# Linear attention beside an FP4 feed-forward, one core: x's transposes on the DMA queue instead of TensorE, and three elementwise jobs off VectorE

## What is computed

```
xn = layernorm(x)                       # x: 8 sequences x 2048 tokens x 256
qkv = xn @ W_qkv.T                      # 16 heads of 16
q = softmax(q over the head) * 16**-0.5;  k = exp(k)
# buckets of 64 tokens: each bucket's q meets the running sums over all earlier buckets
den  = q . cumsum(sum k);  context = cumsum(k^T v);  attn = (q @ context) / max(den, 1e-6)
attention = attn @ W_out.T
# fp4: blocks of 16 are divided by their scale (max|.|/6), rounded to the E2M1 grid, multiplied back
gate, up = fp4(xn) @ fp4(w_gate).T, fp4(xn) @ fp4(w_up).T     # 704 columns each
down = fp4(silu(gate) * up) @ fp4(w_down).T
out = x + attention + down
```

## Time and profile before

| | |
|---|---|
| time, median of 3 runs | 1378.86 us (1377.84 to 1379.21) |
| profiled execution: its time, its span | 1378.78 us, 1377.1 us |
| TensorE matmul busy | 1301.7 us, 95% |
| VectorE busy | 1294.4 us, 94% |
| ScalarE busy | 1028.2 us, 75% |
| GpSimd busy | 250.1 us, 18% |
| granted TensorE clock, mean | 0.989 of full |
| DMA engines, mean busy share | 39.6% in the main queue |

### The profile page before, as it was taken

The page is one execution under the profiler, slowest core; times in us unless marked ns, Lnnn a source line. Parts: engine busy times, 40 slices in busy tenths (PEclk is TensorE's granted clock), DMA queues, the critical chain, the costliest instruction groups (busy, mean ns, idle before and its releaser), DMA issues.

```text
span 1377.1 us, 41687 instructions
## 1 busy us (share of the span) xinstructions
PE 1301.7 (95%) x10318; PEld 913.1 (66%) x10318; DVE 1294.4 (94%) x3901; ACT 1028.2 (75%) x3349; POOL 250.1 (18%) x664
## 2 busy tenths in 40 slices
PE   0279999999999999999999999999999999999996
PEld 0257676677767677676767677676766767676674
DVE  6769999999999999999999999999999999999996
ACT  1577778777787878777787877778787777878772
POOL 2211212111121211112121111112111111212110
PEclk9889999999999999999999999999999999999998
DMA  4023444444344444334444433434444343434334
GB/s 124 4 38 64 91 89 84 88 93 87 78 102 87 84 89 95 83 80 95 92 85 88 97 83 81 99 85 84 88 98 89 76 96 85 92 81 99 81 69 89
DMA packets 362747, 116.85 MB, mean 85 GB/s; under 512 B 327772, under 2 KB 362204, under 8 KB 362716
## 3 DMA queue, kind: packets, MB, share of 16 engines
q1 hardware_dynamic: 361990, 115.80, 39.6%
q10 hardware_dynamic: 726, 0.72, 0.2%
HBM read 19.99 MB, written 16.78 MB: 27 GB/s over the span
## 4 chain that ended last, share of the span: by engine, by line
PE 92%; DVE 4%; ACT 1%; issue 1%; DMA 1%; SPq 0%; DVEq 0%; ACTq 0%
PE outp L1168 11%; PE nump L1118 6%; PE unit1a L1058 6%; PE unit0a L1058 6%; PE outp L1170 5%; PE unit1a L1060 5%; PE unit1a L1062 5%; PE unit0a L1060 5%; PE unit0a L1062 5%; PE ctxp L1128 4%; PE unit1b L1058 4%; PE unit1b L1060 4%; PE unit1b L1062 4%; PE unit0b L1058 4%; PE unit0b L1060 4%; PE unit0b L1062 4%
## 5 line engine op out<-in xcount | busy, mean ns | idle before, releaser
L1168 PE MATMUL outp<-w_down_cat,q_rows 128*128 128x256 f16 x1408 | 246.0, 274 | 0.0
L599 ACT ACTIVATE snap<-ctxp,mask 64x68 f32<-64x68 f32 x1024 | 236.1, 308 | 3.2
L409 POOL TENSOR_TENSOR var_scaled<-squares,var_mul 128x1 f32<-128x1 f32 x128 | 33.5, 262 | 947.8 <-ACT scratch L492 947.8
L1168 PEld LDWEIGHTS outp<-w_down_cat,q_rows 128*128 128x128 f16 x1408 | 138.3, 98 | 16.5
L1170 PE MATMUL outp<-w_down_lo,q_rows 128*128 128x256 f16 x640 | 147.6, 274 | 0.0
L517 ACT ACTIVATE xnt<-trp 128x256 f16<-128x256 f32 x256 | 97.3, 380 | 58.5 <-PE trp L1082 58.5
L562 ACT ACTIVATE th<-unit1a,c_g 128x352 f32<-128x352 f32 x128 | 70.9, 554 | 83.8 <-PE unit1b L1062 83.8
L562 ACT ACTIVATE th<-unit0a,c_g 128x352 f32<-128x352 f32 x128 | 71.0, 555 | 83.0 <-PE unit0b L1062 81.8
L810 DVE TENSOR_REDUCE blk<-h 128x44 f32<-128x704 f32 x128 | 123.8, 967 | 0.1
L863 DVE TENSOR_TENSOR hx_v<-h,blk 128x704 f32<-128x704 f32 x128 | 112.1, 876 | 0.0
L400 POOL TENSOR_TENSOR att_s<-att,att_s 128x256 f16<-128x256 f32 x128 | 86.5, 676 | 124.2 <-ACT att_s L554 124.2
(11 more groups left out here) (203 smaller groups left out, 4156.4 us busy)
## 6 DMA issues: line engine op xcount, KB each, us to landing
xring<-x SPq DMA_DIRECT2D x128, 128.0 KB, 2.7
out<-xring SPq DMA_DIRECT2D x128, 128.0 KB, 2.5
xqt<-xq_s SPq DMA_TRANSPOSE x128, 2.4
att_t<-att_s SPq DMA_TRANSPOSE x128, 2.5
q_rows<-q_rows SPq DMA_TRANSPOSE x128, 3.6
raw_qkv<-wqkv_t SPq DMA_DIRECT2D x1, 768.0 KB, 4.3
raw_up<-wup ACTq DMA_DIRECT2D x2, 352.0 KB
raw_gate<-wgate SPq DMA_DIRECT2D x2, 352.0 KB
```

The lines of the kernel that those rows point to most:

```text
L599: nc.scalar.activation(kept[:, :, cols], sums[:, :, cols], ACT.Copy, scale=mask[rows, f, h:h + 1])\
L1168: nc.tensor.matmul(downp, hqt[:, par, m, :], w_down_cat[:, m, :], start=(m == 0), stop=False)
```

## The change

- TensorE loses `transpose_xn` and `less_xn`. ScalarE instead copies `xn` to fp16 (`high_xn`, new buffer `xn_s`), GpSimd subtracts for the low half (`low_xn`), and the SP queue transposes both halves with one DMA (`turn_xn`), as a fourth transpose for each tile. `transpose_q` no longer waits for x's halves.
- `scale_x` goes from VectorE to GpSimd as it stands.
- VectorE's first addition is split: ScalarE writes attp x c_o into a new SBUF buffer `att_o` (`scale_att`), GpSimd adds x to it (`add_x`), giving `osum`; VectorE keeps the second addition, which now waits for GpSimd.
- Semaphore counts change to match (`xq_step` has 4 steps for each tile and not 6, `o_step` 1 and not 2). `minus16` goes.

```
+            def turn_xn(t, par):
+                sp.wait_ge(xn_lo, after(t))
+                sp.sem_inc(sp_turn, 1)
+                if begun(t - 2):
+                    sp.wait_ge(qkv_done, after(t - 2))
+                sp.sem_inc(sp_turn, 1)
+                sp.dma_start_transpose(xnt[:, par, :, :].rearrange("p s (c k) -> p (s c) k", k=P),
+                                       xn_s[:, par, :, :].rearrange("p s k -> p (s k)")).then_inc(xn_turned[par], 16)
...
                     turn_h(2 * i + d - 1, 1 - d)
+                    turn_xn(2 * i + d + 3, 1 - d)
...
+            def low_xn(t, par):
+                pool.wait_ge(xn_hi, after(t))
+                nc.gpsimd.tensor_tensor(xn_s[:, par, 1, :], xn[:, par, :], xn_s[:, par, 0, :], ALU.subtract).then_inc(xn_lo, 1)
+
+            def scale_x(t, par):
+                rows = lambda ap: ap.rearrange("p (o c) -> p o c", c=2 * XB)
+                pool.wait_ge(hx_step, t * 3 + 3)
+                pool.wait_ge(xq_step, after(t, 4))
+                if begun(t - 2):
+                    pool.wait_ge(xqt_done[par], turned(t - 2, par))
+                nc.gpsimd.tensor_tensor(rows(xq_s[:, par, 0, :]), rows(hx_q[:, F:F + D].bitcast(fp16)), over_pairs(xs_hi[:, :]), ALU.mult)\
+                    .then_inc(xq_made, 1)
+                nc.gpsimd.tensor_tensor(rows(xq_s[:, par, 1, :]), rows(hx_q[:, F:F + D].bitcast(fp16)), over_pairs(xs_lo[:, :]), ALU.mult)\
+                    .then_inc(xq_made, 1)
+
+            def add_x(n, d):
+                t = 2 * n + d
+                pool.wait_ge(att_scaled, after(t))
+                if begun(t - 2):
+                    pool.wait_ge(o_step, after(t - 2))
+                nc.gpsimd.tensor_tensor(osum[:, d % 2, :], att_o[:, :], xring[:, (n + d // 2) % XCH, d % 2, :], ALU.add)\
+                    .then_inc(x_added, 1)
...
                 k, par, odd = 2 * n + d, d, 1 - d
+                scale_x(k + 1, odd)
+                add_x(n, d - 3)
                 low_att(k - 1, odd)
+                low_xn(k + 3, odd)
                 rstd_of(k + 4, par)
...
-            def split_xnt(t, par, part):
-                act.wait_ge((xnt_tr, xnt_less)[part], after(t))
-                if part == 0 and begun(t - 2):
-                    act.wait_ge(qkv_done, after(t - 2))
-                nc.scalar.activation(xnt[:, par, part, :], tr32, ACT.Copy).then_inc(xnt_split, 1)
+            def high_xn(t, par):
+                act.wait_ge(xn_done, after(t))
+                if begun(t - 2):
+                    act.wait_ge(xn_turned[par], turned(t - 2, par))
+                nc.scalar.activation(xn_s[:, par, 0, :], xn[:, par, :], ACT.Copy).then_inc(xn_hi, 1)
...
+            def scale_att(t):
+                act.wait_ge(proj_done, after(t))
+                if begun(t - 1):
+                    act.wait_ge(x_added, after(t - 1))
+                nc.scalar.activation(att_o[:, :], attp, ACT.Copy, scale=c_o[:, :]).then_inc(att_scaled, 1)
...
                 high_att(k - 1, odd)
                 exp_k(k + 1, odd)
+                scale_att(k - 3)
                 exp_q(k + 1, odd)
                 scales_x(k + 2)
                 scales_h(k - 1)
                 tanh_gate(k, 0, par)
-                split_xnt(k + 2, par, 0)
                 normalise_waits(k + 3)
                 mean_waits(n, d + 4)
-                split_xnt(k + 2, par, 1)
                 tanh_gate(k, 1, par)
                 factor_of_row(k - 1, odd)
                 normalise(n, d + 3)
                 mean_of(n, d + 4)
+                high_xn(k + 3, odd)
                 squares_wait(k + 4)
                 copy_qt(k + 1, odd)
                 squares_of(n, d + 4)
...
-            def add_up(n, d, part):
+            def add_up(n, d):
                 t = 2 * n + d
                 if not is_tile(t):
                     return
                 here = xring[:, (n + d // 2) % XCH, d % 2, :]
-                if part == 0:
-                    dve.wait_ge(proj_done, after(t))
-                    if begun(t - 2):
-                        dve.wait_ge(o_step, after(t - 2, 2))
-                    nc.vector.scalar_tensor_tensor(osum[:, d % 2, :], attp, c_o[:, :], here, ALU.mult, ALU.add)\
-                        .then_inc(o_step, 1)
-                else:
-                    dve.wait_ge(o_step, after(t, 2, 1))
-                    dve.wait_ge(c_row_done, after(t))
-                    nc.vector.scalar_tensor_tensor(here, downp, c_row[:, d % 2, :], osum[:, d % 2, :], ALU.mult,
-                                                   ALU.add).then_inc(o_step, 1)
+                dve.wait_ge(x_added, after(t))
+                dve.wait_ge(c_row_done, after(t))
+                nc.vector.scalar_tensor_tensor(here, downp, c_row[:, d % 2, :], osum[:, d % 2, :], ALU.mult, ALU.add)\
+                    .then_inc(o_step, 1)
 
             def step(n, d):
                 k, par, odd = 2 * n + d, d, 1 - d
-                scale_x(k + 1, odd)
...
-                add_up(n, d - 3, 0)
                 round_hx(k - 1, k + 2, 1)
-                add_up(n, d - 3, 1)
+                add_up(n, d - 3)
...
-            def transpose_xn(t, par):
-                pe.wait_ge(xn_done, after(t))
-                if begun(t - 2):
-                    pe.wait_ge(qt_done, after(t - 2))
-                elif t > 0:
-                    pe.wait_ge(xnt_split, after(t - 1, 2))
-                for c in range(KC):
-                    last = nc.tensor.matmul(tr32[:, c * P:(c + 1) * P], xn[:, par, c * P:(c + 1) * P], ident32[:, :],
-                                            start=(c == 0), stop=False, is_transpose=True, skip_group_check=True)
-                last.then_inc(xnt_tr, 1)
-
-            def less_xn(t, par):
-                pe.wait_ge(xnt_split, after(t, 2, 1))
-                nc.tensor.matmul(tr32, minus16[:, :], xnt[:, par, 0, :], start=False, stop=True, skip_group_check=True)\
-                    .then_inc(xnt_less, 1)
...
-                pe.wait_ge(xnt_split, after(t + 1, 2))
+                if begun(t - 1):
+                    pe.wait_ge(qt_done, after(t - 1))
...
                 gate_up(k, 0, par)
-                transpose_xn(k + 2, par)
-                gate_up(k, 1, par, (0,))
-                less_xn(k + 2, par)
-                gate_up(k, 1, par, (1,))
+                gate_up(k, 1, par)
                 transpose_q(k + 1, odd)
```

More of the change, by code:

```diff
@@ L191, in linear_attention_fp4_ffn_block @@
         xn_done = sem("xn_done")
-        xnt_tr = sem("xnt_tr")
-        xnt_split = sem("xnt_split")
-        xnt_less = sem("xnt_less")
+        xn_hi = sem("xn_hi")
+        xn_lo = sem("xn_lo")
+        xn_turned = [sem(f"xn_turned{par}") for par in range(2)]
         qkv_done = sem("qkv_done")
@@ L296, in turn_xq @@
                     return
-                sp.wait_ge(xq_step, after(t, 6))
+                sp.wait_ge(xq_made, after(t, 2))
                 sp.sem_inc(sp_turn, 1)
@@ L324, in turn_att @@
                                        att_s[:, par, :, :].rearrange("p s k -> p (s k)")).then_inc(att_turned[par], 16)
+            def turn_xn(t, par):
+                if not is_tile(t):
+                    return
+                sp.wait_ge(xn_lo, after(t))
[5 more added lines that the diff above has]
+                                       xn_s[:, par, :, :].rearrange("p s k -> p (s k)")).then_inc(xn_turned[par], 16)
             def turn(i):
@@ L341, in _ @@
                 load(0, n)
+            turn_xn(0, 0)
             turn(-1)
@@ L500, in normalise_waits @@
                 if begun(t - 2):
-                    act.wait_ge(xnt_tr, after(t - 2))
+                    act.wait_ge(xn_lo, after(t - 2))
                 if begun(t - 2):
-                    act.wait_ge(xq_step, after(t - 2, 6, 3))
+                    act.wait_ge(xq_step, after(t - 2, 4, 3))
             def normalise(n, d):
@@ L567, in scales_x @@
                     return
-                act.wait_ge(xq_step, after(t, 6, 2))
+                act.wait_ge(xq_step, after(t, 4, 2))
+                if begun(t - 1):
+                    act.wait_ge(xq_made, after(t - 1, 2))
                 nc.scalar.activation(xs_hi[:, :].rearrange("p (b i) -> p b i", i=2), twice(xblk[:, 1, :]), ACT.Copy)\
@@ L576, in factor_of_row @@
                 if begun(t - 2):
-                    act.wait_ge(o_step, after(t - 2, 2))
+                    act.wait_ge(o_step, after(t - 2))
                 nc.scalar.activation(c_row[:, par, :], hrow[:, 1, :], ACT.Copy, scale=c_d[:, :]).then_inc(c_row_done, 1)
@@ L824, in block_scales @@
                 if is_tile(u):
-                    dve.wait_ge(xq_step, after(u, 6, 1))
+                    dve.wait_ge(xq_step, after(u, 4, 1))
                     nc.vector.tensor_scalar(xblk[:, 1, :], xblk[:, 0, :], SIX_TIE * 2.0 ** 11, XS * TINY * 2.0 ** 11, ALU.mult, ALU.max)\
@@ L839, in over_one @@
                     if do_x:
-                        dve.wait_ge(xq_step, after(u, 6, 2))
```

(21 more changed lines are left out.)

24 lines of the change are left out of this document (14 added, 10 removed).

## The result

The changed kernel takes 1454.17 us (median of 4 runs, 1453.15 to 1457.57) against 1379.03 for the kernel before on the same chip: ratio 1.0549 [1.0529, 1.0569], 75 us slower. The prediction said 1374, at most 1402. Its rival 3 had the direction.

The account below looks back on a forecast made before the run. TensorE bounds before, VectorE nearly as full; afterwards VectorE bounds at 8.90 + 0.5 + 0.5 + 0.1 = 10.00 us a tile. TensorE's gain of 0.33 shrinks to 0.05: 6 us less, 1 more, so 1374 us, range 1340 to 1402.

Parts of the forecast that it names:

- rival 3: Slower: `scale_x` products cost VectorE a third full collision or last longer and reach L863; 1397 to 1422 us, chance 0.30.
- TensorE minus 0.33, ScalarE level with it: Without x's transposes and `less_xn` TensorE takes 9.72 us a tile; ScalarE's snapshot path comes to 9.74.
- the bound without collisions: The time if GpSimd's operations keep no VectorE operation out: 1338 us.
- The 0.1 us to wake TensorE: Allowance between the end of ScalarE's snapshot and TensorE's start, about 0.1 us.
- The removed first addition, minus 0.40: VectorE loses its first addition, counted by starts as 0.40 us less for each tile.
- `scale_x`, 0.1: GpSimd's two products near the next Q (start of `bucket`) delay VectorE's two small scale operations by 0 to 0.5, taken 0.1.
- VectorE would drift past: Argument against rival 3: a later VectorE drifts past the products of `scale_x`.
- `add_x`, 0.5: GpSimd's `add_x` gets in between VectorE's L863 and the rounding L870, making L870 0.5 us late.
- `low_att`, 0.5: GpSimd's `low_att`, now behind `add_x`, starts inside the delayed L870 and makes the rounding L884 0.5 us late.
- the forecast's 10.00: VectorE's sum for one tile in us: 8.90 + 0.5 + 0.5 + 0.1.
- Rival 3's condition: Rival 3 decides from 1.15 us of VectorE delays for each tile on; 1.5 us gives 1422 us.
- The collision's price: Each full collision of a full-width GpSimd operation with a VectorE operation costs 0.5 us, even between back-to-back operations.

Follow-up runs that it names:

- e7: x's transposes off TensorE, `scale_x` on GpSimd one step earlier, let go by VectorE's last product of h; both additions as in the kernel before: 1334.32 us, ratio 0.9679.
- e14: e7 with VectorE's second addition moved behind `gate_h` and `low_scales`, same operations on the same engines: 1382.98 us, ratio 1.0036.
- e5: The changed kernel with VectorE's `gate_h` of the first half moved between the two rounding operations: 1436.58 us, ratio 1.0414.
- e6: The changed kernel with `low_att` put ahead of `scale_x` and `add_x` in GpSimd's step: 1391.87 us, ratio 1.0097.
- e3: The changed kernel with both additions back on VectorE, without `scale_att` and `add_x`: 1354.90 us, ratio 0.9824.
- e9: The changed kernel with only the two products of `scale_x` moved one step earlier, behind the last reading of hx_q: 1395.51 us, ratio 1.0117.
- e11: The kernel before plus one unused full-width GpSimd addition for each tile, let go by the reciprocal ahead of the rounding: 1401.29 us, ratio 1.0171.
- e8: The kernel before plus one unused full-width GpSimd addition for each tile, let go by ScalarE's copies of v: 1380.01 us, ratio 1.0006.
- e12: The kernel before plus one unused full-width GpSimd addition for each tile, let go by VectorE's last product of h: 1379.96 us, ratio 1.0008.
- e4: The changed kernel with x's transposes back on TensorE, without `high_xn`, `low_xn` and the fourth DMA transpose: 1430.93 us, ratio 1.0375.
- e10: The changed kernel with `scale_x` placed one step earlier, `low_att` first in GpSimd's step and `gate_h` between the rounding operations: 1370.89 us, ratio 0.9950.

## Why the prediction was wrong

The mechanism and its places were right; two terms of VectorE's sum failed, a third was somewhat too large, and the argument that kept rival 3 small failed with them.

- **TensorE minus 0.33, ScalarE level with it: right.** e7 runs at 9.68 a tile with TensorE full, against the predicted 9.72, and at 1334 where the bound without collisions was 1338. (The 0.1 us to wake TensorE stood on no row; from VectorE's end to TensorE's start e14 has 0.15.)
- **The removed first addition, minus 0.40: the step that failed most clearly.** It was counted by its own starts. It stood between two operations of which the second needs the first's result; without it VectorE waits there for 0.33. The removal was worth 0.06. Shown by L949's wait, by e5, where that wait is gone, and by e6, where it stays though the collision ahead of it is gone. The Trainium skill ("VectorE: DVE Perf Modes", Rules for kernel authors) advises to minimise the number of VectorE operations and not the semaphores; here the trace differs, since one operation less left 0.33 of its 0.39 us as a wait, and of the 0.24 us in which VectorE stands idle there 0.18 pass in the sequencer instructions of two further semaphore waits.
- **`scale_x`, 0.1: it measured 0.61.** The place was right within some 0.3 us (predicted from Q + 9.5, which is 0.5 ahead of the next Q at the forecast's 10.0 a tile; found from 702.08, 0.76 ahead of the `bucket` at 702.84), and that 0 to 0.5 could be lost there stood in the text. I took the low end because VectorE would drift past. It does not: GpSimd's work is let go by VectorE and ScalarE of the same step, so the two keep their places in every tile, and L887 pays the same in all 84 tiles (721 to 725 ns). With two products and two small operations there are also two hits, not one. e3 (the products alone hit them) and e9 (placed, the loss is gone) show it.
- **`add_x`, 0.5: right**, 0.53. **`low_att`, 0.5: 0.35.**
- **Together:** the forecast's 10.00, plus 0.33 and 0.51, less 0.15, and less 0.05 for the start (VectorE's own 9.68 and not 9.72) and small things, is 10.64, as measured.
- **Rival 3's condition was met**: it decided from 1.15 us of delays; there were 0.53 + 0.35 + 0.61 = 1.49, near its upper price of 1.5 (1422). The gap, which no rival had, is 0.33 x 124 = 41 us, more than the 32 by which that was exceeded.
- **The collision's price, called the weakest point, held.** The rows of the kernel before had it from operations that start behind GpSimd's; e11 has 0.39 for one let go shortly ahead of its victim, the changed kernel 0.35 to 0.53. The Trainium skill ("SBUF — State Buffer", Who interferes with whom) has operations with one SBUF input outside the two-port modes and reductions free of it, and here the trace agrees: in e8 L771 kept 0.41 us beside the spare addition, and in e12 the two operations beside it, with an input in PSUM each, kept their 0.46 and 0.41.

What stays open: why the products hold up the first small operation for longer in e5, and whether VectorE's wait on its own result would shrink with its three waits in another order. Whether `low_xn` alone makes the difference of 23 us in e4 was not isolated.

## What to carry to other kernels

Work given to GpSimd is priced by its place, not by its length: list what VectorE does during each of its full-width operations, and let it go with a semaphore at a stretch of PSUM inputs and reductions; in these kernels, whose engines run in lock step, the collisions came back turn after turn (at most they alternated between neighbouring operations), and no drift removed them. Before removing an operation from a full engine, look whether it covers the time between a producer and its consumer, the consumer's further waits included. And where two engines both show waits, look for the loop between them: its length, not either engine's sum, was the time in e10 and e14, and moving independent work out of it cost nothing.

## What the hardware showed that was not expected

- VectorE on its own result: the rounding operation L949, which needs the one before it and has two more waits behind the wait for it, starts 0.24 us after its end (707.40 to 707.63); L941, whose wait for the operation before it is its last, starts 0.03 after that one's end; an independent operation behind L941 starts 0.08 ahead of its end (e5: 700.69, where the rounding began at 699.76 and lasted 1.01).
- Where GpSimd is let go inside an operation of VectorE both engines pay: `add_x` took 1.18 to 1.35 us and L927 0.94; apart 0.73 and 0.42. Where it starts just ahead of its victim VectorE alone pays: in e11 the spare addition kept its 0.73.
- A GpSimd product of 128x256 in fp16 with its second operand repeated over pairs takes 0.67 us, as does `low_att`, a plain difference with an fp16 result; the spare addition, fp32 throughout, takes 0.73.
